# Adding routed expert rows into a token-ordered DRAM buffer by accumulating DMA, with layer 1's setup weights fetched during the experts

## The reference

```python
x = x + L0_xattn(layernorm(x), ctx)        # 16 heads of 64, low-rank terms, 73 + 4 keys
x = x + L0_ffn(layernorm(x))
x = x + L1_xattn(layernorm(x), ctx)        # 8 heads of 32, 77 keys
x = x + L1_ffn(layernorm(x))               # 8 experts, width 256, top 2

# L0_ffn
gates = softmax(relu(xf @ Wr1 + br1) @ Wr2 + br2)
tg, ti = top_k(gates, 2);  tg = softmax(tg / 2)
out = silu(xf @ Ws1 + bs1) @ Ws2 + bs2                  # shared expert
for e in range(8):                                      # width 1024
    h = silu(xf @ We1[e] + be1[e]) @ We2[e] + be2[e]
    out = out + sum(tg * (ti == e))[:, None] * h
```

## Time and profile before

| | |
|---|---|
| median of 3 runs | 1066.58 us (1061.05 to 1068.49) |
| the profiled execution | 1069.34 us, its span 1067.5 us |
| PE, DVE, ACT, POOL busy | 90%, 67%, 45%, 13% of the span |
| DMA | 111.57 MB, mean 105 GB/s |
| mean granted TensorE clock | 0.945 of full speed |

### The profile page before, as it was taken

One profiled execution on the slowest core, in us unless ns is written; L12 is line 12 of the kernel. 1 busy time (PEld: TensorE's weight loads), 2 busy tenths in 40 slices (PEclk: granted clock), 3 DMA queues, 4 the chain that ended last, 5 costly groups with the idle time before them and its releaser, 6 DMA issues. The chain is left out here.

```text
span 1067.5 us, 18419 instructions
## 1 busy us (share of the span) xinstructions
PE 960.9 (90%) x6397; PEld 870.8 (82%) x6397; DVE 720.3 (67%) x1262; ACT 483.1 (45%) x897; POOL 142.2 (13%) x128
## 2 busy tenths in 40 slices
PE   4998889999768999999999999966499779999998
PEld 3776679998548999999999999933388747899998
DVE  2334388998429988778877887667587676555665
ACT  0001223333227676667766766401355354455443
POOL 1000022233002860000000000037022100000000
PEclk9999999999858999999999999966699989999999
DMA  8800000000037865665566556033000020000002
GB/s 232 302 0 1 1 1 1 1 1 1 3 97 284 308 240 216 229 239 196 198 238 237 211 198 244 21 107 104 6 1 1 1 80 21 20 21 20 20 2 79
DMA packets 44276, 111.57 MB, mean 105 GB/s; under 512 B 7460, under 2 KB 29702, under 8 KB 35526
## 3 DMA queue, kind: packets, MB, share of 16 engines
q1 hardware_dynamic: 34902, 96.55, 25.6%
q0 software_dynamic: 3072, 8.39, 2.3%
q10 hardware_dynamic: 6256, 6.03, 1.8%
HBM read 90.51 MB, written 18.35 MB: 102 GB/s over the span
## 5 line engine op out<-in xcount | busy, mean ns | idle before, releaser
L93 PE MATMUL e_ps_h<-e_xh,e_w1h 128*128 128x256 f32 x496 | 144.4, 291 | 0.3 <-issue 0.3
L95 PE MATMUL e_ps_h<-e_xh,e_w1l 128*128 128x256 f32 x496 | 141.7, 286 | 0.0
L94 PE MATMUL e_ps_h<-e_xl,e_w1h 128*128 128x256 f32 x496 | 141.7, 286 | 0.0
L93 PE MATMUL e_ps_o<-e_w2h,e_hh 128*128 128x256 f32 x496 | 140.4, 283 | 0.0
L94 PE MATMUL e_ps_o<-e_w2l,e_hh 128*128 128x256 f32 x496 | 140.4, 283 | 0.0
L95 PE MATMUL e_ps_o<-e_w2h,e_hl 128*128 128x256 f32 x496 | 140.4, 283 | 0.0
L1447 ACT ACTIVATE e_hf<-e_ps_h,e_b1s 128x256 f32<-128x256 f32 x248 | 104.2, 471 | 40.8 <-PE e_ps_h L95 33.8
L659 POOL TENSOR_TENSOR at_pr<-at_pr,at_inv 128x1168 f32<-128x1168 f32 (+2 forms) x48 | 58.6, 1235 | 299.2 <-DVE at_inv L606 299.2
L93 PEld LDWEIGHTS e_ps_h<-e_xh,e_w1h 128*128 128x128 f32 x496 | 96.7, 195 | 0.5 <-issue 0.5
L94 PEld LDWEIGHTS e_ps_h<-e_xl,e_w1h 128*128 128x128 f32 x496 | 96.8, 195 | 0.0
L95 PEld LDWEIGHTS e_ps_h<-e_xh,e_w1l 128*128 128x128 f32 x496 | 96.5, 195 | 0.0
(11 more groups left out here) (252 smaller groups left out, 2399.6 us busy)
## 6 DMA issues: line engine op xcount, KB each, us to landing
e_w1s<-in_m_w SPq DMA_DIRECT2D x31, 1024.0 KB
e_w2s<-in_m_w SPq DMA_DIRECT2D x31, 1024.0 KB
slots_in<-zero SPq DMA_DIRECT2D x23, 256.0 KB, 6.5
e_xin<-slots_in SPq DMA_DIRECT2D x23, 256.0 KB
slots_out<-e_yo ACTq DMA_DIRECT2D x23, 256.0 KB, 4.8
X<-in_x SPq DMA_DIRECT2D x1, 2048.0 KB, 24.0
e_xin<-m_xn SPq DMA_DIRECT2D x8, 256.0 KB
d_w1s<-in_m_w SPq DMA_DIRECT2D x8, 256.0 KB, 2.7
```

The costliest lines, as they stand in the source:

```text
L93: nc.tensor.matmul(out, lh, rh, start=start, stop=False)
L94: nc.tensor.matmul(out, lh, rl, start=False, stop=False)
L95: return nc.tensor.matmul(out, ll, rh, start=False, stop=stop)
```

## The change

The slot rows get 258 columns: 256 of data, the token number (column `TOKEN`), the gate (`GATE`). POOL scatters the 16 tiles of the first choice, waits until they have landed, copies the second gates into the column, and scatters the other 16. DVE copies the two extra columns of every routed tile out of `xin`, and the refill of `xin` waits for DVE (`s_xlo`) instead of PE (`s_tr`). ACT stores the finished shared tiles of `g.X` to a new DRAM buffer `accumulated` (`g.acc`). For a routed tile, ACT multiplies `yo` by the gates in place (two instructions) and no longer stores it. POOL then adds its two halves onto `g.acc` by indirect DMA with an add, each issued only when the one before has landed. Layer 1's nine operands are loaded by SP after step S into the space of `m.xn`. In the setup SP waits for the last two tiles' adds and reads `g.X` back in four DMAs; `add_tile` is only `bn_stats` and no longer runs in the first head group; POOL sets `vbd` and `row` to zero. `Combine` is gone.

```diff
@@ scatter @@
-    for t in range(NT):
-        for i in range(TOPK):
+    for i in range(TOPK):
+        pool.wait_ge(router.s_k, i + 1)
+        if i:
+            pool.wait_ge(m.s_sc, 16 * NT * i)
+            nc.gpsimd.tensor_copy(m.xn[:, :, GATE], router.gates[:, i, :]).then_inc(s_gate, 1)
+            pool.wait_ge(s_gate, i)
+        for t in range(NT):
             nc.gpsimd.indirect_dma_start(
                 out=g.xs, out_offset=bass.IndirectOffsetOnAxis(ap=m.slots[:, i, t:t + 1], axis=0),
                 in_=m.xn[:, t, :], in_offset=None).then_inc(m.s_sc, 16)
@@ experts, gpsimd @@
+                pool.wait_ge(s_acc, 16 * S)
+                for n in range(ROUTED):
+                    pool.wait_ge(s_ys, n + 1)
+                    for a in range(ROWS):
+                        before = n * ROWS + a - 1
+                        if before >= 0:
+                            q = before // ROWS % 2
+                            pool.wait_ge(s_st[q], 16 * (before // ROWS // 2 * ROWS + before % ROWS + 1))
+                        nc.gpsimd.indirect_dma_start(
+                            out=g.acc, out_offset=bass.IndirectOffsetOnAxis(ap=token[:, n, a:a + 1], axis=0),
+                            in_=yo[:, n % 2, a, :], in_offset=None, compute_op=ALU.add).then_inc(s_st[n % 2], 16)
@@ experts, sync @@
-                            wait(sp, s_tr, j - 1)
+                            wait(sp, s_xlo, j - 1)
-                steps(sp, make(False), S, J + 1, (S + 1, J - 2))
+                make(False)(S, S % 2)
+                early.load(sp)
+                steps(sp, make(False), S + 1, J + 1, (S + 1, J - 2))
@@ experts, scalar @@
+                        if shared and not static or static and 0 <= j - 2 < S:
+                            wait(act, s_sx, j - 1)
+                            rows = g.acc[0:TOK].rearrange("(j a p) d -> j p a d", p=P, a=ROWS)
+                            t = (j - 2) * ROWS
+                            if static:
+                                act.dma_start(rows[j - 2], g.X[:, t:t + ROWS, :]).then_inc(s_acc, 16)
...
+                        elif not static or j - 2 >= S:
                             wait(act, s_ev, j - 1)
-                            act.dma_start(rows, yo[:, q]).then_inc(s_st[q], 16)
+                            for a in range(ROWS):
+                                last = nc.scalar.activation(yo[:, q, a, :], yo[:, q, a, :], ACT.Copy,
+                                                            scale=gate[:, n, a:a + 1] if static else gate[:, bass.ds(n, 1), a:a + 1])
+                            last.then_inc(s_ys, 1)
-                for n in (ROUTED - 2, ROUTED - 1):
-                    act.wait_ge(s_st[n % 2], arrived(n, n % 2))
@@ experts, vector @@
+                                for dst, col in ((token, TOKEN), (gate, GATE)):
+                                    nc.vector.tensor_copy(dst[:, n, :] ..., xin[:, 1 - q, :, col])
                             nc.vector.tensor_tensor(xl[:, 1 - q], ps_x[:, 1 - q], xh[:, 1 - q], ALU.subtract).then_inc(s_xlo, 1)
...
-                                    wait(dve, s_st[1 - q], arrived(n, 1 - q))
+                                    wait(dve, s_st[1 - q], ROWS * arrived(n, 1 - q))
@@ attention_setup @@
-                if before:
-                    before.gather(pool)
+                if early:
+                    for zeros in (vbd[:], g.row[:].bitcast(FP)):
+                        nc.gpsimd.memset(zeros, 0.0).then_inc(s_zero, 1)
-                    for zeros in (kbd[:], vbd[:], g.row[:].bitcast(FP)):
-                        nc.vector.memset(zeros, 0.0).then_inc(s_zero, 1)
+                    nc.vector.memset(kbd[:], 0.0).then_inc(s_zero, 1)
-                            if before or gi > 0:
+                            if gi > 0:
                                 add_tile()
+                while added[0] < NT:
+                    add_tile()
@@ Combine -> Reload @@
+    def sync(self, sp):
+        for n in (ROUTED - 2, ROUTED - 1):
+            sp.wait_ge(self.m.s_st[n % 2], 16 * ST // P * (n // 2 + 1))
+        rows = self.g.acc[0:TOK].rearrange("(t p) d -> p t d", p=P)
+        each = NT // self.PARTS                                        # PARTS = 4
+        for i, s in enumerate(self.s_x):
+            ts = slice(i * each, (i + 1) * each)
+            sp.dma_start(self.g.X[:, ts, :], rows[:, ts, :]).then_inc(s, 16)
+    def add(self, dve, t):
+        if t % each == 0:
+            dve.wait_ge(self.s_x[t // each], 16)
+        self.nc.vector.bn_stats(self.g.stats[:, t, :], self.g.X[:, t, :]).then_inc(self.s_bn, 1)
+class Early:                     # nine tiles laid over m.space, the SBUF of m.xn
+    def load(self, sp):
+        for names, loaded in ((("ctx",), self.s_w), (("wk", "bk"), self.s_wk), (("wv", "bv"), self.s_wv),
+                              (("wq", "wo", "bo", "bq"), self.s_wq)):
+            for name in names:
+                sp.dma_start(self.tiles[name][:], self.w[name]).then_inc(loaded, 16)
```

More of the change, by code:

```diff
@@ L206, in attention_setup @@
         pb = lambda name, shape: ctx.enter_context(nc.psum_tensor(T + name, shape, FP))
[L207 to L213, removed]
+        if early:
+            c, wk, wv, wq, wo, bo, bq, bk, bv = (early.tiles[n] for n in ("ctx", "wk", "wv", "wq", "wo", "bo", "bq", "bk", "bv"))
+            s_w, s_wk, s_wv, s_wq = early.s_w, early.s_wk, early.s_wv, early.s_wq
+            n_w, n_wk, n_wv, n_wq = 1, 2, 2, 4
+        else:
+            c = sb("ctx", [CP, CK, NB, KEYS])
+            wk, wv = sb("wk", [CP, CK, HD]), sb("wv", [CP, CK, HD])
+            wq, wo = sb("wq", [P, G, D]), sb("wo", [P, G, D])
+            bo = sb("bo", [1, D])
+            s_w, s_wk, s_wv, s_wq = (sem(T + n) for n in ("context_loaded", "wk_loaded", "wv_loaded", "wq_wo_loaded"))
             ci = sb("ctx_ipa", [CP, CK, NB, KEYS])
-            loads.append((ci, w["ctx"]))
             wki, wvi = sb("wki", [CP, CK, HD]), sb("wvi", [CP, CK, HD])
@@ L252, in _ @@
             def _(sp):
-                for group, loaded in ((loads, s_w), (loads_k, s_wk), (loads_v, s_wv), (loads_lq, s_lq), (loads_q, s_wq)):
+                groups = () if early else ((loads, s_w), (loads_k, s_wk), (loads_v, s_wv), (loads_lq, s_lq), (loads_q, s_wq))
+                for group, loaded in groups:
                     for dst, src in group:
@@ L266, in _ @@
             def _(pe):
-                pe.wait_ge(s_w, 16 * len(loads))
+                pe.wait_ge(s_w, 16 * n_w)
                 if L.lora:
@@ L1268, in scatter, with experts @@
                 in_=m.xn[:, t, :], in_offset=None).then_inc(m.s_sc, 16)
-def experts(nc, g, m, L, w, sem, router, idle):
+def experts(nc, g, m, L, w, sem, router, idle, early):
     T = f"e{L.n}_"
@@ L1278, in experts @@
     s_b1, s_b2 = sem(T + "b1_loaded"), sem(T + "b2_loaded")
-    s_st = [sem(f"{T}stored{q}") for q in range(2)]
+    s_st = m.s_st = [sem(f"{T}stored{q}") for q in range(2)]
     s_w1h, s_w1l, s_w2h, s_w2l = sem(T + "w1_high"), sem(T + "w1_low"), sem(T + "w2_high"), sem(T + "w2_low")
@@ L1369, in step @@
                                 rows = rows[j - S] if static else rows[bass.ds(j - S, 1)].rearrange("j p a d -> p (j a) d")
-                            sp.dma_start(xin[:, q], rows).then_inc(s_xl[q], 16)
+                            sp.dma_start(xin[:, q, :, 0:D] if shared else xin[:, q], rows).then_inc(s_xl[q], 16)
                         if not static or 1 <= j <= J:
@@ L1478, in step @@
                             wait(dve, s_xh, j + 2)
+                            if not shared or static and j + 1 >= S:
+                                n = j + 1 - S
+                                for dst, col in ((token, TOKEN), (gate, GATE)):
+                                    nc.vector.tensor_copy(dst[:, n, :] if static else dst[:, bass.ds(n, 1), :].rearrange("p n a -> p (n a)"),
+                                                          xin[:, 1 - q, :, col])
                             nc.vector.tensor_tensor(xl[:, 1 - q], ps_x[:, 1 - q], xh[:, 1 - q], ALU.subtract).then_inc(s_xlo, 1)
@@ L1573, in mixture @@
         m.s_sc = sem(f"m{L.n}_scattered")
-        experts(nc, g, m, L, w, sem, router, idle)
+        experts(nc, g, m, L, w, sem, router, idle, early)
         for h in idle:
```

161 lines of the change are left out of this document (83 added, 78 removed).

## The result

The changed kernel takes 1088.3 us (median of four runs, 1081.9 to 1090.1) against 1067.5 us for the kernel before beside it: ratio 1.0182, 95% interval 1.0142 to 1.0222. It is slower by about 20 us, where I had forecast 15 us less. A second comparison gave 1.0187 (1.0152 to 1.0222).

The account below looks back on a forecast made before the run. PE was taken to bound the experts, the gather chain the 58.2 us setup. Later start +5.0, setup -20.1, experts 0: -15.1 us from the profiled 1069.3, 1054.2; less 2.8 to the median, rounded to 1052; range 1043 to 1070.

Parts of the forecast that it names:

- The length L of an add: POOL's add chain: issue to next issue taken as 3.4 us, near the plain scatter's 2.4; bounds 2.4 to 6.
- The adds under the experts: Experts: two adds per tile take 8.4 us, fit into PE's 11.9 us period, and so cost zero.
- The shut-out: Experts: weight loads keep POOL's DMAs off the DMA engines, as with the scatters, for 4 to 5 us per tile.
- Rival 1: Experts: adds don't keep pace, POOL sets the pace from L = 5.95; at L = 7 +44 us, 1111 us; chance 0.13.
- The tail: End of the experts: the last serial adds lie bare, so the setup starts 5.0 us later.
- The scatters and early loads: Tiles 8 and 9: middle scatter wait and nine early loads delay SP's loads; taken as zero, upper bound 5 us.
- rival 3: Tiles 8 and 9: longer scatter and early loads make PE wait, 5 to 8 us, 1059 us; chance 0.10.
- The setup: Layer 1's setup: without gathers and adds, a PE, ACT and DVE chain of 38 us replaces 58.2.
- rival 4: Setup: PE's clock is granted in full, 6 us off, total 1046 us; chance 0.12.
- Rival 2: Setup: ACT's 14.32 us hold comes back or another wait replaces it, about 8 us on the path, 1060 us; chance 0.13.
- What I costed at nothing: Experts: ACT's scaling (0.9 us per tile), DVE's two copies (under 0.2 us each) and `xin`'s wait for `s_xlo` cost zero.

Follow-up runs that it names:

- pairs: Changed kernel with a tile's two adds issued one behind the other, waiting only for the previous tile's two: 1055.2 us, ratio 0.9832 to the kernel before.
- pairs of adds and the split wait: Changed kernel, adds waiting only for the previous tile's two, second gates written per eight landed scatters: 1046.4 us, ratio 0.9785; again 1047.8, 0.9847.
- pairs, split and 264 columns: Same as pairs of adds and the split wait, but slot rows of 264 columns in place of 258: 1052.0 us, ratio 0.9831; again 1053.4, 0.9878.

## Why the prediction was wrong, step by step

- **The length L of an add**, from its issue to the next one's, is the step that failed. I put it at 3.4 us, "near the scatter, since the two differ in nothing that the program issues", between 2.4 and 6. Alone it is 3.9 to 4.6 us; a plain write over the same rows is 2.66. The addition has three times the packets and 0.6 us more of issue. The two do differ in what the program issues: one adds. Under a weight load L is 9.07, outside my bounds, which I had taken from scatters landing in quiet.
- **The adds under the experts.** I reckoned 5 + 3.4 = 8.4 us a tile and took zero. It is 4.1 + 9.07, or 13.15 with the decimals. The shut-out was foreseen in its kind, but the sum let it stand in place of the shut-out add's own length. A shut-out comes on top: 5 + 3.4 + 3.4 would have been 11.8, at the edge of the 11.9 at hand, even with my L. The longer issue (3.12) was not foreseen at all. Rival 1 is what came: 46 adds in 281 us, 6.25 us each on average, past the 6.0 from which I had said it decides. Its formula with 6.25 puts the setup 30 us late; it was 48 us late, since the first add also came at 461.2, not 448.9, and the block's end took longer. The price under the experts is 25 us by the kernel without adds.
- **The tail**: 5.0 us forecast, 17.0 measured. I let the chain reach the third last tile without a backlog. It was behind by a tile when the last `yo` was written, so four adds followed it, at distances of 4.2 us on average; and the block's end took 5.7 us in place of 0.65, of which 2.8 also came where POOL was last without any add.
- **The scatters and early loads** (rival 3): 6.7 us from tile 5's `xh` to tile 9's, of which I had named 5 as the upper bound and taken zero. The middle wait caused it; the nine loads did not.
- **The setup**: 20.1 us less forecast, 25.9 measured. The walk through it was right in its steps (PE at work 0.2 us after the start; no statistics waiting for the reload, which landed in 6 us). B's products began 17.9 us into the block (18.65 in the walk) and ran at a granted clock of 1.00: it is the bound that I had put at 6 us off, and rival 4. Rival 2, ACT's hold coming back, did not happen; what had held ACT before stays open.
- **What I costed at nothing** and was nothing: ACT's scaling (0.91 us for two, no table load), DVE's copies, SP's other wait. Without adds the period is 11.7 us.

With pairs the adds are hidden as the forecast had them, and the time is 1055 us, where it had 1052. That this comes so near is partly luck: the start of the setup after the last `yo` moved by 8.9 us and not by 5.0, the four tiles up to tile 9 took 6.3 us more and not zero, and the setup became 27 us shorter and not 20. The direction was lost on one term.

The best version measured has pairs of adds and the split wait: 1046.4 and 1047.8 us in two comparisons, 1.5 to 2.2% under the kernel before, where the changed kernel is 1.8% over it.

## What to carry to other kernels

A chain of DMAs in which each waits for the landing of the one before is an engine of its own that no busy time shows: price one link under the heaviest traffic that it will meet, sum a period, and compare that with the period of the bound engine. Put a shut-out on top of the link's own length, not in its place. If the links needn't be ordered (here the two halves of a tile), issue them together before anything else is tuned. And don't price an accumulating DMA by a plain one. A difference of a few us between two traces, ahead of all that was edited, can belong to the execution: trace the same kernel twice before explaining it.

## What was unexpected of the hardware

- An accumulating indirect DMA of 128 rows of 1 KB: 1.56 us of issue, 144 packets, 4.1 us from issue to issue; the plain one 0.96 us, 48 packets, 2.66 us.
- An experts' block whose last engine is POOL ended 3.04 us after the last result, without any DMA; with POOL long done, 0.26 us.
- The same matrix products at granted clock 1.00 (but for the group of `xh` with `w1h`, which reads some 5 ns more) took 283 ns on average in the kernel before, 279 to 282 with rows of 258 columns and 281 to 282 with 264. In the group below it is 283, 279 or 280, and 281 or 282. Between the kernels with pairs and split only the rows' length differs, and with it where the tiles lie in SBUF; that the place is the cause is not shown. It makes 3.1 us over 30 tiles (343.5 against 346.6), and 0.2 us a tile against before, a gain that the change brought by the way. From 470 to 496 us, the group of `ps_h` products of `xl` in the kernel before, with pairs, and with pairs, split and 264 columns:

```profile
L94 PE MATMUL e_ps_h<-e_xl,e_w1h 128*128 128x256 f32 x35 | 9.9, 283 | 0.0
```

```profile
L96 PE MATMUL e_ps_h<-e_xl,e_w1h 128*128 128x256 f32 x33 | 9.2, 279 | 0.0
```

```profile
L96 PE MATMUL e_ps_h<-e_xl,e_w1h 128*128 128x256 f32 x32 | 9.0, 282 | 0.0
```
